# An adaLN and mixture-of-experts block on one core: recurrence steps and residual transposes moved between the output matmuls

## The chip, the cores and the metric

One core of a Trainium2 chip runs the whole block as one program. The metric is device time in microseconds. The program is written engine by engine: TensorE (PE), VectorE (DVE), ScalarE (ACT), GpSimd (POOL) and SyncE (SP) each have their own instruction list, and they meet at semaphores.

## The reference

Two layers follow each other on x of shape (16, 128, 128), 2048 tokens of 128 features.

```python
x = x + ffn0(cond0(x, cond, weight), w_gate, w_up, w_down)
x = x + ffn1(cond1(x, cond, Wx, Wh, b), router_w, w1, b1, w2, b2)

# ffn0: every tensor is quantised to 16 bits with one scale from its largest magnitude
up, gate = act_qdq(x @ up.T), act_qdq(x @ gate.T)
gate = act_qdq(gate * fixed_qdq_u16(sigmoid(gate)))
o = act_qdq(gate * up)
return o @ dequant(w_down).T

# cond1: a recurrence over 128 times, 16 batches side by side
next_h = tanh(xw_t + prev_h @ Wh)

# ffn1: 8 experts of width 512, the best 2 of each token mixed by softmax
h1 = gelu(x @ w1.T + b1);  expert = h1 @ w2.T + b2
```

## The kernel before

Values are kept as pairs of float16 numbers (high and low part), and a product is three or four float16 matmuls, so that nearly float32 accuracy is kept. The 128 times are cut into five chunks of 256, 384, 512, 512 and 384 tokens (`WIDTHS`; below, chunks 0 to 4, "the third chunk" is chunk 2). Both the output of the first layer and the loop of the second go chunk by chunk.

The change touches the stage between the two layers. Its steps for chunk c are:

- Quantise: `quantise_o` on VectorE multiplies the product `up2` by a scale and adds `MAGIC` (line 744, float32 to float32 in place, semaphore `oq`); the rounded 16-bit number then stands in the low bytes. The high byte becomes float16 in `o_hi` (line 746, VectorE). The low byte becomes float16 in `o_lo` through `low_byte`, on ScalarE for the first `LOW_SCALAR` = 3 chunks (line 543) and on GpSimd for the other two (line 393).
- Output: twelve matmuls on TensorE (lines 1031 to 1040) multiply high and low part by the high and low weights; matmuls 0 to 5 need `o_hi`, 6 to 11 need `o_lo` too. Line 893 is the helper that issues every matmul.
- Residual: `make_x1` (line 752, VectorE) scales the output out of PSUM and adds the transposed x; `split_x1` makes the float16 pair (cast, line 759; subtraction, line 761).
- Recurrence: `first_step` on TensorE is a float32 product of `Wh` with the last state, 16 columns; ScalarE's `first_step` takes the tanh (line 555), and the next step waits for it. The first 16 steps (`FIRST_STEPS`) belong to chunk 0 and run in this stage: `input_part` puts the input product of these steps in PSUM, then steps stand after every third output matmul from chunk 2 on (`STEP_EVERY`), and what is left comes behind the last chunk. GpSimd splits the states (lines 404 and 406) and then prepares the bias b2 (lines 411 to 414).
- Residual in token order: `transpose_x1` (line 1017) transposes all sixteen residual tiles behind the steps, four to a PSUM bank. ScalarE copies two banks into the accumulator `acc` (line 563), VectorE the other two (line 779).

Then the loop over experts begins (`pair`): eight slots to an iteration, in each a hidden product on TensorE, Gelu on ScalarE (lines 592 and 594), the float16 pair on VectorE (cast 868, subtraction 872), and from the fifth slot on the down product of the slot four before, for which TensorE waits on `g_lo_done`. Recurrence steps of the next chunk stand between the slots.

The engines' own lists set the order: VectorE goes through quantise 0, quantise 1, residual and split 0, quantise 2, quantise 3, residual and split 1, quantise 4, residual and split 2, residual 3, residual 4, split 3, the bank copies, split 4.

Of the kernel before, what the change touches and what calls it, by code (L numbers as in the profile page):

```python
# [8 lines left out]
ALU = mybir.AluOpType  # L9
ACT = mybir.ActivationFunctionType  # L10
X, XY = mybir.AxisListType.X, mybir.AxisListType.XY

P = 128
B = 16
# [3 lines left out]
NJ = INNER // P  # L18
BANK = 512
NK = TOK // BANK  # L20
# [10 lines left out]
FIRST_STEPS = WIDTHS[0] // B  # L31
RNN_SLOTS = ((0, 1, 3, 4, 5, 7), range(8), range(8), (0, 1, 2, 4, 5, 6), ())
RNN_FROM = [FIRST_STEPS + E // 2 * sum(len(n) for n in RNN_SLOTS[:c]) for c in range(CH)]
# [6 lines left out]
MAGIC = 12582912.0  # L40
# [2 lines left out]
C_SCALAR = (0, 2)  # L43
W_POOL = 8
WARM = 14
STEP_EVERY = 3
LOW_SCALAR = 3
W0_AT = (0, 3, 14)
WY_V = 10
TIMES = [s // B for s in START]  # L50
W_CHUNKS = 2 * E
BH_LO = 32
ACC_SCALAR = 2
CHUNK_OF = [c for c in range(CH) for _ in range(TILES[c])]
LAST_SYNC, LAST_SCALAR = (0, 2), (1,)
LATE = NK - ACC_SCALAR
# [5 lines left out]
def program(nc, x, cond, w_cond, w_gate, w_up, w_down, w_x, w_h, b_h, w_router, w1, b1, w2, b2, out):  # L62
    ctx = ExitStack()
    with ctx:
# [9 lines left out]
        banks = [ctx.enter_context(nc.psum_tensor(f"bank{i}", [P, BANK], F32)) for i in range(8)]  # L74


        ident = sb("ident", [P, P])
# [22 lines left out]
        gate2, up2, sig2 = (big[:, i * NJ * TOK:(i + 1) * NJ * TOK] for i in range(3))  # L100
# [3 lines left out]
        sc = sb("sc", [P, 5, 5])  # L104
# [46 lines left out]
        wt_t = [sem(f"wt_t{i}") for i in range(2)]  # L151
# [64 lines left out]
        def chunk_of(t, c):  # L216

            return t.rearrange("p (jb t) -> p jb t", t=T)[:, :, TIMES[c]:TIMES[c + 1]]
# [5 lines left out]
        def by_batch(c):  # L224

            return banks[DOWN_BANKS[c]][:, 0:WIDTHS[c]].rearrange("p (b t) -> p b t", b=B)
# [222 lines left out]
        def _(act):  # L449
# [91 lines left out]
            def low_byte(c):  # L541
                act.wait_ge(oq, c + 1)
                A(chunk_of(o_lo, c), chunk_of(up2.bitcast(U8)[:, 0::4], c), ACT.Copy).then_inc(o_lo_done, 1)
# [2 lines left out]
            weight_lo(W_CHUNKS - 1)  # L546
            for c in range(1, LOW_SCALAR):
                low_byte(c)
            act.wait_ge(misc_sb, 1)

            def first_step(r):

                act.wait_ge(rnn_mm, r + 1)
                at = slice(r * B, (r + 1) * B)
                A(h32[:, at], ps_rnn[:, at], ACT.Tanh, scale=1 / WS).then_inc(h32_done, 1)  # L555


            act.wait_ge(wt_t[1], 16 * (W_CHUNKS - W_POOL))
            for r in range(FIRST_STEPS):
                first_step(r)  # L560
            for k in range(ACC_SCALAR):
                act.wait_ge(x1T_mm, k + 1)
                A(acc[:, 4 * k:4 * k + 4, :].rearrange("p j h -> p (j h)"), banks[ACC_BANKS[k]][:, :],
                  ACT.Copy).then_inc(acc_s, 1)
# [41 lines left out]
        def _(dve):  # L606
# [134 lines left out]
            peak_to_scale(4, 2 * NJ, lambda u: link(V.tensor_tensor(u, sc[:, 3, 2:3], sc[:, 2, 2:3], ALU.mult)))  # L741
            def quantise_o(c):

                V.tensor_scalar(chunk_of(up2, c), chunk_of(up2, c), sc[:, 4, 4:5], MAGIC, ALU.mult, ALU.add).then_inc(oq, 1)  # L744
                dve.wait_ge(oq, c + 1)
                V.tensor_scalar(chunk_of(o_hi, c), chunk_of(up2.bitcast(I8)[:, 1::4], c), 256.0, None,  # L746
                                ALU.mult).then_inc(o_hi_done, 1)
# [143 lines left out]
        def _(pe):  # L891
            def mm(o, l, r, start, stop=True):
                return nc.tensor.matmul(o, l, r, start=start, stop=stop, skip_group_check=True)  # L893
# [101 lines left out]
            def input_part(first, to):  # L995

                at = slice(B * first, B * to)
                o = ps_rnn[:, 0:B * (to - first)]
                mm(o, bh_rows[:, :], ones[:, 0:B * (to - first)], True)
                mm3(o, wx_hi[:, :], wx_lo[:, :], x1_hi[:, at], x1_lo[:, at], False)  # L1000
# [3 lines left out]
            def first_step(r):  # L1004

                if r:
                    pe.wait_ge(h32_done, r)
                state = h32[:, B * (r - 1):B * r] if r else yT[:, :]
                mm(ps_rnn[:, B * r:B * (r + 1)], w_h32, state, False).then_inc(rnn_mm, 1)

            def transpose_x1(k):

                pe.wait_ge(x1_done, k + 2)
                for j in range(4 * k, 4 * k + 4):
                    last = nc.tensor.transpose(banks[ACC_BANKS[k]][:, P * (j % 4):P * (j % 4 + 1)], x1[:, P * j:P * (j + 1)],  # L1017
                                               ident[:, :])
                last.then_inc(x1T_mm, 1)

            step = 1
            for c in range(CH):
                if c == 2:
                    pe.wait_ge(w_lo_s, W_CHUNKS - W_POOL)
                    pe.wait_ge(small_w, 2)
                    pe.wait_ge(bh_ready, 1)
                    pe.wait_ge(x1_lo_done, 1)
                    input_part(0, FIRST_STEPS)
                    first_step(0)
                pe.wait_ge(o_hi_done, c + 1)  # L1030
                for p, (part, w) in enumerate(((o_hi, wT_hi), (o_hi, wT_lo), (o_lo, wT_hi), (o_lo, wT_lo))):
                    if p == 2:
                        pe.wait_ge(*((o_lo_done, c + 1) if c < LOW_SCALAR else (o_lo_p, c + 1 - LOW_SCALAR)))
                    for j in range(NJ):
                        if c >= 2 and (NJ * p + j) % STEP_EVERY == 1 and step < FIRST_STEPS:
                            first_step(step)
                            step += 1
                        last = mm(by_batch(c), w[:, 2 * NJ + j, :], chunk_of(part, c)[:, B * j:B * (j + 1), :],
                                  p == 0 and j == 0)
                last.then_inc(down_mm, 1)  # L1040

            for r in range(step, FIRST_STEPS):
                first_step(r)
            for k in range(NK):
                transpose_x1(k)

            def transpose_gates(c):

# [50 lines left out]
            def pair(c, e2, prev):  # L1099
                first = is_first(e2)  # L1100
                for s in range(2 * NF):
                    f = s % NF
                    if 0 < c < CH - 1 and first and s == 0:
                        pe.wait_ge(h32_done, RNN_FROM[c])
                        pe.wait_ge(x1_lo_done, CH)
                        input_part(RNN_FROM[c], RNN_FROM[c + 1])

                    if first and s == 0:
                        earlier_slot(c, e2, prev, s)
                    step = rnn_step(c, e2, s)  # L1110
                    if c == 0 and first and s in (2, 3):
                        pe.wait_ge(acc_s, s - 1)
                    if c == 0 and first and s == NF:
                        pe.wait_ge(added, 1)
                    if first and s == 0:
                        pe.wait_ge(h_lo_done, START[c + 1] // (4 * B))

                    if prev or s >= NF:
                        slot = c * SLOTS + e2 * 2 * NF + s
                        two_reads = f in HI_SCALAR[c] or (first and f in HI_SCALAR[c - 1])  # L1120
                        pe.wait_ge(g_lo_done if two_reads else g32_done, slot - NF + 1)
                    t = slice(START[c], START[c + 1])
                    o, w_hi, w_lo = ps_h[f][:, 0:WIDTHS[c]], *(wt_flat[:, w_cols(e2, s, 0, low)] for low in range(2))
                    mm(o, w_hi, h_hi[:, t], True)
                    mm(o, w_lo, h_hi[:, t], False)
                    if step is not None:
                        pe.wait_ge(h32_done, step)
                        mm(ps_rnn[:, bass.ds(rnn_column(c, step), B)], w_h32, h32[:, bass.ds((step - 1) * B, B)],
                           False).then_inc(rnn_mm, 1)
                    mm(o, w_hi, h_lo[:, t], False).then_inc(hid_mm, 1)  # L1130
                    if not (first and s == 0):
                        earlier_slot(c, e2, prev, s)
                    if first and s == 0:
                        if prev:
                            pe.wait_ge(logit_sb, c)
                        logits(c)
                    if first and c > 0 and s == 4:
                        transpose_gates(c - 1)
                    if first and c > 0 and s == 6:
                        mix_b2(c - 1)  # L1140
                    if isinstance(e2, int) and not first and s == 2:
                        transpose_gates(c)
                    if isinstance(e2, int) and not first and s == 4:
                        mix_b2(c)

            pe.wait_ge(h32_done, FIRST_STEPS)
            pe.wait_ge(x1_lo_done, 2)
            input_part(FIRST_STEPS, RNN_FROM[1])
            pe.wait_ge(wt_t[0], 16 * W_POOL)
            pe.wait_ge(wt_t[1], 16 * (W_CHUNKS - W_POOL))  # L1150
            chunks(pe, pair)
# [22 lines left out]
```

## Time and profile before

| | |
|---|---|
| median of 3 runs | 302.65 us (301.67 to 302.88) |
| span of the profiled execution | 301.2 us |
| median less span | 1.45 us |
| PE busy | 264.4 us, 88% |
| DVE busy | 258.8 us, 86% |
| ACT busy | 215.6 us, 72% |
| POOL busy | 76.2 us, 25% |
| stage between the layers | about 81 to 104 us of the span |

The span runs from the first to the last instruction of one profiled execution; its record gives no other time for that execution. Busy shares are of the span. In a timeline a row is a group of like instructions: start, length, engine, line, operation, output and input, shapes, count; square brackets give the idle time ahead of it and who ended it. The names in rows are those of the underlying buffers: `big` holds up2 and the hidden values, `x_sb` the residual's float16 pair, `c` the residual, `wyT` the accumulator, `q` the recurrence states.

### The profile page before, as it was taken

The numbers are of one execution on the slowest core, as the hardware profiler recorded it, in microseconds if no ns is written. First come the engines' busy times: TensorE is split into PE (matmuls) and PEld (weight loads), VectorE is DVE, ScalarE is ACT, GpSimd is POOL, SyncE is SP. The second block draws the span as 40 slices with busy tenths as digits, with TensorE's granted clock in tenths as the row PEclk, the third lists the DMA queues.
The fourth block names the chain that finished last, engine by engine and source line by source line (L and its number), as shares of the span: only waits on it lengthen the run. The fifth ranks groups of instructions, "written<-read, shape, count | busy, mean of one in ns | idle before, by whom it ended". The sixth has DMA issues, their size and how long they took to land.

```text
span 301.2 us, 8834 instructions
## 1 busy us (share of the span) xinstructions
PE 264.4 (88%) x2716; PEld 205.5 (68%) x2716; DVE 258.8 (86%) x635; ACT 215.6 (72%) x455; POOL 76.2 (25%) x148
## 2 busy tenths in 40 slices
PE   4969940049989999999999999999999999999994
PEld 4824440016956777778888788888777887888874
DVE  4888999989898897779988799887799988889885
ACT  6367899998842677767777676667566766689892
POOL 3367997000025413011302112212110311101000
PEclk9989976557999999999999999999999999999999
DMA  6990443101500000000000000000001000001000
GB/s 186 314 310 4 84 94 76 28 0 35 90 17 2 0 3 1 0 2 2 19 0 0 2 3 26 2 0 0 1 2 30 8 0 0 2 1 37 0 2 27
DMA packets 24031, 10.63 MB, mean 35 GB/s; under 512 B 13355, under 2 KB 22982, under 8 KB 24006
## 3 DMA queue, kind: packets, MB, share of 16 engines
q1 hardware_dynamic: 23470, 10.05, 13.6%
q10 hardware_dynamic: 536, 0.26, 0.3%
q8 instruction: 14, 0.23, 0.3%
q14 instruction: 11, 0.09, 0.1%
HBM read 6.11 MB, written 1.05 MB: 24 GB/s over the span
## 4 chain that ended last, share of the span: by engine, by line
PE 79%; DVE 16%; issue 1%; ACT 1%; DMA 1%; SPq 0%; DVEq 0%
PE bank L893 78%; DVE peak L706 3%; DVE big L728 3%; DVE peak L633 2%; DVE big L711 1%; DVE big L744 1%; PE bank L937 1%; DMA y_sb<-in_cond 1%; PE bank L1017 0%; DVE big L746 0%; DVE wyT L779 0%; DVE pkm L626 0%; DVE big L738 0%; DVE x_sb L759 0%; DVE q L700 0%
## 5 line engine op out<-in xcount | busy, mean ns | idle before, releaser
L893 PE MATMUL bank<-big,wt 128*128 128x384 f16 (+2 forms) x480 | 124.8, 336 | 0.6 <-DVE big L872 0.5
L893 PE MATMUL bank<-wt,big 128*128 (+1 forms) x1536 | 111.5, 219 | 0.1
L872 DVE TENSOR_TENSOR big<-big 128x384 f16<-128x384 f32 (+2 forms) x160 | 93.2, 585 | 20.5 <-ACT big L594 16.1
L893 PEld LDWEIGHTS bank<-wt,big 128*128 128x128 f16 x1536 | 97.9, 97 | 16.2 <-issue 0.2
L592 ACT ACTIVATE big<-bank,miscT 128x384 f32<-128x384 f32 (+2 forms) x160 | 96.2, 602 | 15.3 <-PE bank L893 8.2
L893 PEld LDWEIGHTS bank<-q,wxh 128*128 128x128 f32 x254 | 44.4, 189 | 17.4 <-issue 3.4
L893 PEld LDWEIGHTS bank<-big,wt 128*128 (+1 forms) x480 | 50.0, 117 | 4.8 <-issue 1.1
L580 ACT ACTIVATE q<-bank (+1 forms) x112 | 20.6, 184 | 38.7 <-PE bank L893 37.9
L404 POOL CAST big<-q 128x64 f16<-128x64 f32 x32 | 13.2, 413 | 129.0 <-ACT q L580 126.5
L868 DVE CAST big<-big 128x512 f16<-128x512 f32 (+2 forms) x104 | 38.6, 372 | 4.8 <-ACT big L592 3.9
L827 DVE SCALAR_TENSOR_TENSOR wyT<-bank,gates,wyT 128x128 f32<-128x128 f32 x128 | 39.8, 343 | 1.0 <-issue 0.6
L893 PE MATMUL bank<-q,wxh 128*128 (+1 forms) x254 | 38.9, 228 | 1.1 <-ACT q L555 0.7
L594 ACT ACTIVATE big<-bank,miscT 128x384 f16<-128x384 f32 (+2 forms) x56 | 33.1, 590 | 0.0
L893 PE MATMUL bank<-ident,pk 128*128 128x128 f32 x10 | 2.9, 378 | 20.6 <-DVE pk L621 20.6
L893 PE MATMUL bank<-q,wT_hi 128*128 128x512 f16 x48 | 15.8, 398 | 3.0 <-DVE q L698 2.4
L893 PEld LDWEIGHTS bank<-ident,pk 128*128 128x128 f32 x10 | 2.0, 237 | 21.7 <-DVE pk L621 17.4
L506 ACT ACTIVATE big<-bank 128x512 f32<-128x512 f32 x24 | 14.0, 602 | 3.5 <-PE bank L893 2.9
L633 DVE TENSOR_REDUCE peak<-big 128x1 f32<-128x1024 f32 x12 | 14.6, 1219 | 0.4
L706 DVE TENSOR_REDUCE peak<-big 128x1 f32<-128x1536 f32 x8 | 14.0, 1745 | 0.4 <-ACT big L506 0.2
L393 POOL CAST big<-big 128x1536 f16<-128x1536 uint8 (+1 forms) x2 | 3.9, 1962 | 38.9 <-DVE big L744 38.9
L406 POOL TENSOR_TENSOR big<-q,big 128x64 f16<-128x64 f32 x32 | 12.6, 395 | 2.6
L893 PEld LDWEIGHTS bank<-q,wT_hi 128*128 128x128 f16 x48 | 4.8, 101 | 9.8 <-issue 4.1
(165 smaller groups left out, 320.0 us busy)
## 6 DMA issues: line engine op xcount, KB each, us to landing
wnat<-in_w SPq DMA_DIRECT2D x8, 512.0 KB, 7.7
x_sb<-in_x SPq DMA_DIRECT2D x4, 256.0 KB, 4.3
out_block<-wyT SPq DMA_DIRECT2D x15, 64.0 KB
wn<-in_w_gate ACTq DMA_DIRECT2D x1, 192.0 KB, 4.9
wn<-in_w_up SPq DMA_DIRECT2D x1, 192.0 KB, 5.6
wn<-in_w_down SPq DMA_DIRECT2D x1, 192.0 KB, 5.7
b_in<-in_b SPq DMA_DIRECT2D x12, 4.0 KB
wt<-wyT SPq DMA_TRANSPOSE x8, 3.0
```

The source lines that it names most:

```text
L404: G.tensor_copy(h_hi[:, at], h32[:, at]).then_inc(h_hi_done, 1)
L406: G.tensor_tensor(h_lo[:, at], h32[:, at], h_hi[:, at], ALU.subtract).then_inc(h_lo_done, 1)
L506: A(blk(t, j * NK + k), banks[GU_BANKS[n % 5]][:, :], ACT.Copy).then_inc(gu_sb, 1)
L580: A(h32[:, bass.ds(step * B, B)], ps_rnn[:, bass.ds(rnn_column(c, step), B)], ACT.Tanh, scale=1 / WS).then_inc(h32_done, 1)
L592: A(g32[:, f, 0:w], ps_h[f][:, 0:w], ACT.Gelu, bias=bias, scale=1 / WS).then_inc(g32_done, 1)
L594: A(g_hi[:, s // NF, f, 0:w], ps_h[f][:, 0:w], ACT.Gelu, bias=bias, scale=1 / WS).then_inc(g_hi_done, 1)
L633: link(V.tensor_reduce(peak[:, i, n:n + 1], t, X, ALU.max, apply_absolute_value=True))
L706: link(V.tensor_reduce(peak[:, i, k:k + 1], tokens((gate2, up2)[i - 1], k), XY, ALU.max, apply_absolute_value=True))
L827: V.scalar_tensor_tensor(a, ps_y[par][:, P * j:P * (j + 1)], g, a, ALU.mult, ALU.add).then_inc(added, 1)
L868: V.tensor_copy(g_hi[:, par, f, 0:w], g32[:, f, 0:w]).then_inc(hi_v, 1)
L872: V.tensor_tensor(g_lo[:, par, f, 0:w], g32[:, f, 0:w], g_hi[:, par, f, 0:w], ALU.subtract).then_inc(g_lo_done, 1)
L893: return nc.tensor.matmul(o, l, r, start=start, stop=stop, skip_group_check=True)
```

## The change

On TensorE, `STEPS_AT` lists before which output matmuls of each chunk a recurrence step stands: step 0 (with the input part) before matmul 9 of chunk 1, six in each of chunks 2 and 3, three in chunk 4. From matmul 1 of chunk 3 on each step is followed by one transpose of a residual tile, eight in all; tiles 8 to 11 come behind chunk 4, then the input part of the next steps (which stood just before the loop), then tiles 12 to 15. On ScalarE the low byte of chunk 2 goes, and its quantising comes; the wait for the weights' transposes moves behind the steps; it copies three banks, VectorE one. GpSimd takes the low bytes of chunks 2, 3 and 4.

```diff
--- before.py
+++ after.py
@@ -43,14 +43,16 @@
 C_SCALAR = (0, 2)
 W_POOL = 8
 WARM = 14
-STEP_EVERY = 3
-LOW_SCALAR = 3
+STEPS_AT = ((), (9,), (1, 3, 5, 7, 9, 11), (1, 3, 5, 7, 9, 11), (1, 4, 7))
+FILL_FROM = (3, 1)
+Q_SCALAR = 2
+LOW_SCALAR = 2
 W0_AT = (0, 3, 14)
 WY_V = 10
 TIMES = [s // B for s in START]
 W_CHUNKS = 2 * E
 BH_LO = 32
-ACC_SCALAR = 2
+ACC_SCALAR = 3
 CHUNK_OF = [c for c in range(CH) for _ in range(TILES[c])]
 LAST_SYNC, LAST_SCALAR = (0, 2), (1,)
 LATE = NK - ACC_SCALAR
@@ -546,6 +548,7 @@
             weight_lo(W_CHUNKS - 1)
             for c in range(1, LOW_SCALAR):
                 low_byte(c)
+            A(chunk_of(up2, Q_SCALAR), chunk_of(up2, Q_SCALAR), ACT.Copy, scale=sc[:, 4, 4:5], bias=MAGIC).then_inc(oq, 1)
             act.wait_ge(misc_sb, 1)
 
             def first_step(r):
@@ -555,9 +558,9 @@
                 A(h32[:, at], ps_rnn[:, at], ACT.Tanh, scale=1 / WS).then_inc(h32_done, 1)
 
 
-            act.wait_ge(wt_t[1], 16 * (W_CHUNKS - W_POOL))
             for r in range(FIRST_STEPS):
                 first_step(r)
+            act.wait_ge(wt_t[1], 16 * (W_CHUNKS - W_POOL))
             for k in range(ACC_SCALAR):
                 act.wait_ge(x1T_mm, k + 1)
                 A(acc[:, 4 * k:4 * k + 4, :].rearrange("p j h -> p (j h)"), banks[ACC_BANKS[k]][:, :],
@@ -741,7 +744,8 @@
             peak_to_scale(4, 2 * NJ, lambda u: link(V.tensor_tensor(u, sc[:, 3, 2:3], sc[:, 2, 2:3], ALU.mult)))
             def quantise_o(c):
 
-                V.tensor_scalar(chunk_of(up2, c), chunk_of(up2, c), sc[:, 4, 4:5], MAGIC, ALU.mult, ALU.add).then_inc(oq, 1)
+                if c != Q_SCALAR:
+                    V.tensor_scalar(chunk_of(up2, c), chunk_of(up2, c), sc[:, 4, 4:5], MAGIC, ALU.mult, ALU.add).then_inc(oq, 1)
                 dve.wait_ge(oq, c + 1)
                 V.tensor_scalar(chunk_of(o_hi, c), chunk_of(up2.bitcast(I8)[:, 1::4], c), 256.0, None,
                                 ALU.mult).then_inc(o_hi_done, 1)
@@ -1010,39 +1014,46 @@
 
 
 
-            def transpose_x1(k):
-
-                pe.wait_ge(x1_done, k + 2)
-                for j in range(4 * k, 4 * k + 4):
-                    last = nc.tensor.transpose(banks[ACC_BANKS[k]][:, P * (j % 4):P * (j % 4 + 1)], x1[:, P * j:P * (j + 1)],
-                                               ident[:, :])
-                last.then_inc(x1T_mm, 1)
-
-            step = 1
+            def transpose_x1(j):
+
+                if j % 4 == 0:
+                    pe.wait_ge(x1_done, j // 4 + 2)
+                last = nc.tensor.transpose(banks[ACC_BANKS[j // 4]][:, P * (j % 4):P * (j % 4 + 1)], x1[:, P * j:P * (j + 1)],
+                                           ident[:, :])
+                if j % 4 == 3:
+                    last.then_inc(x1T_mm, 1)
+
+            step = filled = 0
             for c in range(CH):
-                if c == 2:
-                    pe.wait_ge(w_lo_s, W_CHUNKS - W_POOL)
-                    pe.wait_ge(small_w, 2)
-                    pe.wait_ge(bh_ready, 1)
-                    pe.wait_ge(x1_lo_done, 1)
-                    input_part(0, FIRST_STEPS)
-                    first_step(0)
                 pe.wait_ge(o_hi_done, c + 1)
                 for p, (part, w) in enumerate(((o_hi, wT_hi), (o_hi, wT_lo), (o_lo, wT_hi), (o_lo, wT_lo))):
                     if p == 2:
                         pe.wait_ge(*((o_lo_done, c + 1) if c < LOW_SCALAR else (o_lo_p, c + 1 - LOW_SCALAR)))
                     for j in range(NJ):
-                        if c >= 2 and (NJ * p + j) % STEP_EVERY == 1 and step < FIRST_STEPS:
+                        if NJ * p + j in STEPS_AT[c]:
+                            if step == 0:
+                                pe.wait_ge(w_lo_s, W_CHUNKS - W_POOL)
+                                pe.wait_ge(small_w, 2)
+                                pe.wait_ge(bh_ready, 1)
+                                pe.wait_ge(x1_lo_done, 1)
+                                input_part(0, FIRST_STEPS)
                             first_step(step)
                             step += 1
+                            if (c, NJ * p + j) >= FILL_FROM and filled < 8:
+                                transpose_x1(filled)
+                                filled += 1
                         last = mm(by_batch(c), w[:, 2 * NJ + j, :], chunk_of(part, c)[:, B * j:B * (j + 1), :],
                                   p == 0 and j == 0)
                 last.then_inc(down_mm, 1)
 
-            for r in range(step, FIRST_STEPS):
-                first_step(r)
-            for k in range(NK):
-                transpose_x1(k)
+            assert step == FIRST_STEPS
+            for j in range(filled, 12):
+                transpose_x1(j)
+            pe.wait_ge(h32_done, FIRST_STEPS)
+            pe.wait_ge(x1_lo_done, 2)
+            input_part(FIRST_STEPS, RNN_FROM[1])
+            for j in range(12, B):
+                transpose_x1(j)
 
             def transpose_gates(c):
 
@@ -1111,7 +1122,7 @@
                     if c == 0 and first and s in (2, 3):
                         pe.wait_ge(acc_s, s - 1)
                     if c == 0 and first and s == NF:
-                        pe.wait_ge(added, 1)
+                        pe.wait_ge(acc_s, ACC_SCALAR)
                     if first and s == 0:
                         pe.wait_ge(h_lo_done, START[c + 1] // (4 * B))
 
@@ -1143,9 +1154,6 @@
                     if isinstance(e2, int) and not first and s == 4:
                         mix_b2(c)
 
-            pe.wait_ge(h32_done, FIRST_STEPS)
-            pe.wait_ge(x1_lo_done, 2)
-            input_part(FIRST_STEPS, RNN_FROM[1])
             pe.wait_ge(wt_t[0], 16 * W_POOL)
             pe.wait_ge(wt_t[1], 16 * (W_CHUNKS - W_POOL))
             chunks(pe, pair)
```

## Rows read from the trace of the kernel before

**Rows 1.** Page: each engine's busy time, share of the span, instructions.

```profile
PE 264.4 (88%) x2716; PEld 205.5 (68%) x2716; DVE 258.8 (86%) x635; ACT 215.6 (72%) x455; POOL 76.2 (25%) x148
```

**Rows 2.** Chain of waits, in order of time: start us, us, what.

```profile
130.26 167.18 PE bank L893 x2006
```

**Rows 3.** Timeline of VectorE, 79.5 to 106: start us, us, engine line op.

```profile
85.40 1.01 DVE L744 TENSOR_SCALAR big<-big,sc 128x1536 f32<-128x1536 f32 x1
86.45 0.96 DVE L746 TENSOR_SCALAR big<-big 128x1536 f16<-128x1536 int8 x1
...
88.38 0.96 DVE L746 TENSOR_SCALAR big<-big 128x1536 f16<-128x1536 int8 x1
...
90.15 0.72 DVE L759 CAST x_sb<-c 128x384 f16<-128x384 f32 x1
...
92.91 1.08 DVE L752 SCALAR_TENSOR_TENSOR c<-bank,pk,xT 128x512 f32<-128x512 f32 x1
...
97.06 0.85 DVE L752 SCALAR_TENSOR_TENSOR c<-bank,pk,xT 128x384 f32<-128x384 f32 x1 [0.87 <-PE bank L893]
97.83 0.41 DVE L759 CAST x_sb<-c 128x512 f16<-128x512 f32 x1
98.28 0.69 DVE L761 TENSOR_TENSOR x_sb<-c,x_sb 128x512 f16<-128x512 f32 x1
...
100.15 1.29 DVE L779 COPY wyT<-bank 128x512 f32<-128x512 f32 x2 [1.18 <-PE bank L1017]
101.36 0.98 DVE L759 CAST x_sb<-c 128x384 f16<-128x384 f32 x1
...
102.84 0.29 DVE L868 CAST big<-big 128x256 f16<-128x256 f32 x1
```

**Rows 4.** Timeline of TensorE, 79.5 to 106.

```profile
84.16 0.66 PE L893 MATMUL bank<-big,wT_hi 128*128 128x384 f16 x3 [0.15 <-DVE big L746]
...
87.47 0.39 PE L893 MATMUL bank<-big,wT_hi 128*128 128x512 f16 x1 [0.41 <-DVE big L746]
...
89.52 0.38 PE L893 MATMUL bank<-big,wT_hi 128*128 128x512 f16 x1
89.73 0.29 PE L893 MATMUL bank<-q,wxh 128*128 128x16 f32 x2
89.87 0.59 PE L893 MATMUL bank<-big,wT_hi 128*128 128x512 f16 x2
...
97.62 0.40 PE L893 MATMUL bank<-q,wxh 128*128 128x16 f32 x2 [0.27 <-ACT q L555]
98.29 0.40 PE L893 MATMUL bank<-q,wxh 128*128 128x16 f32 x2 [0.27 <-ACT q L555]
98.54 1.95 PE L1017 MATMUL bank<-ident,c 128*128 128x128 f32 x16
...
101.18 0.38 PE L893 MATMUL bank<-big,wt 128*128 128x256 f16 x2
...
103.74 0.38 PE L893 MATMUL bank<-big,wt 128*128 128x256 f16 x2 [0.47 <-DVE big L872]
```

**Rows 5.** Timeline of ScalarE, 79.5 to 106: low bytes.

```profile
83.34 1.16 ACT L543 ACTIVATE big<-big 128x1152 f16<-128x1152 uint8 x1
86.45 1.48 ACT L543 ACTIVATE big<-big 128x1536 f16<-128x1536 uint8 x1 [1.95 <-DVE big L744]
```

**Rows 6.** Timelines of GpSimd and VectorE where both are at work.

```profile
46.25 1.16 POOL L351 TENSOR_TENSOR nat<-wnat,nat 128x512 f16<-128x512 f32 x1
46.27 1.68 DVE L711 TENSOR_SCALAR big<-big 128x1024 f32<-128x1024 f32 x1
63.27 0.76 DVE L733 TENSOR_SCALAR big<-big,sc 128x1024 f32<-128x1024 f32 x1
...
88.41 2.25 POOL L393 CAST big<-big 128x1536 f16<-128x1536 uint8 x1 [37.19 <-DVE big L744]
...
100.96 1.15 POOL L414 TENSOR_TENSOR b_diag<-b_in,b_diag 32x512 f16<-32x512 f32 x1
```

## The prediction, made before the changed kernel ran

> **What bounds the kernel now.** I read the page's busy line first: TensorE is busy 88% of the span, VectorE 86%, ScalarE 72%, GpSimd 25% [rows 1]. TensorE is the engine of the span as a whole, but shares are averages over stages, so the next view is the chain of waits. It ends in one unbroken TensorE piece of 167.18 us from 130.26 on [rows 2], and in the stage ahead of the loop, which this change touches, it crosses VectorE for the residual's bank copies and split. The stage ends where the loop's fifth slot starts on TensorE, at 103.74, after 0.47 us of waiting for VectorE's L872 [rows 4]. That slot needs VectorE's first pair (L868 at 102.84, then L872) [rows 3]. The loop's slots are paced alike before and after the change, so every microsecond by which L868 moves should move the end of the kernel by the same amount. The question is only when VectorE reaches its first L868.
>
> Backwards from 102.84, VectorE has: the split of the last residual chunk (from 101.36, its cast alone 0.98), the two copies of residual banks from 100.15, an idle wait of 1.18 us before them for the transposes, and ahead of that the fourth chunk's split (0.41 and 0.69) after the fifth residual chunk (0.85 at 97.06), which itself waits for the last output matmul [rows 3]. So three things hold the stage up: output matmuls, the tail of recurrence steps, the transposes.
>
> The sum is made against the profiled execution, of which the record gives the span, 301.2 us. The median of the timed runs is 302.65 us, 1.45 us more, and I carry that difference over. A change under 0.5% (1.5 us) I call none.
>
> **Term 1, the third chunk's quantising on ScalarE.** ScalarE ends its low byte of the second chunk at 84.50. An operation of the new one's size took 1.48 (the 1536-element low byte at 86.45) [rows 5]. The trace has none of this form and size; I take 1.5, from 84.5 to 86.0, with bounds of 1.2 (the 1.16 of 1152 elements) and 2.0 (a third more). VectorE drops its own 1.01 us (85.40 to 86.41) and its high byte (0.96) runs from 86.05 to 87.0, not from 86.45 to 87.41 [rows 3]. That is 0.4 us earlier. The cover is VectorE's wait of 0.65 us for ScalarE.
>
> **Term 2, the first step in the second chunk.** Nine matmuls of 0.163 us (three of 384 columns in 0.66 with the drain of the last; 0.21 for 512 columns gives 0.16 as well) from 84.16 end at 85.63. The first split residual chunk is there by then, since VectorE goes on to its next operation at 85.40. The input part (four matmuls of 256 columns, about 0.6), step 0 (0.14) and the three matmuls that are left (0.49) end at about 86.9, ahead of the new high byte at 87.0 [rows 3, 4]. So the move costs TensorE nothing. It starts the recurrence 1.3 us earlier, since ScalarE's 1.48 us low byte no longer stands in front of the first tanh. Chunk 2 starts at 87.05 instead of 87.47 [rows 4].
>
> **Term 3, a step every two matmuls.** One 512-column matmul takes 0.21 us of TensorE (89.52 to 89.73) and one step 0.14 (89.73 to 89.87). A step with two matmuls is 0.57. But where a step waits for its tanh the period is 0.67 (97.62 to 98.29), so chunk 2 is bound by the recurrence: 0.2 + 6 x 0.67, ending at 91.25. In chunk 3 a transpose fills the gap: sixteen in 1.95 us is about 0.12 each, so the period is 0.69 and TensorE does not wait. Chunk 4 has 0.75 a step. The three steps exposed behind the last chunk (0.27 us of waiting each) and twelve of the sixteen transposes leave the tail [rows 4].
>
> **Term 4, the low byte on GpSimd.** This is the term that decides. The ordinary length of GpSimd's cast has to be taken apart: it lasts 2.25 us from 88.41, and VectorE's high byte (0.96 at 88.38) runs until 89.34, so 1.32 come after it [rows 3, 6]. That GpSimd and some VectorE operations exclude each other is plain elsewhere. L711 on VectorE, a scalar operation from and to SBUF, took 1.68 us at 46.27 while GpSimd's L351 ran until 47.41; a like one (L733) with GpSimd idle took 0.76 [rows 6]. The cast at 90.15 took 0.72 (384 columns, where 512 took 0.41) and the one at 101.36 took 0.98, both beside GpSimd [rows 3, 6]. In the changed kernel VectorE's quantising of the fourth chunk comes right behind its high byte, at 87.0, exactly where GpSimd's low byte of the third chunk wants the ports. Whichever goes first, one high byte later both are done: 87.0 + 1.2 + 1.0 + 0.96 = 90.15, against 89.34 before. That is 0.8 us later. The low byte is ready at 88.3 to 89.3, and TensorE asks for it at about 89.
>
> The Trainium skill's page "GPSIMD Engine Reference", section "Specifications", says that GpSimd shares its SBUF interfaces with VectorE and contends with its two-port modes and with operations that have two SBUF inputs. The trace agrees in the 1.68 us above; without that rule the result would be the first rival's below.
>
> **Term 5, the residual and TensorE's wait for it.** From the fourth high byte to the end of the third residual chunk there were 4.65 us (89.34 to 92.91 + 1.08) [rows 3]; these operations stay, so it ends at 94.8. TensorE's fifth filled-in transpose needs it, and comes at 91.25 + 0.21 + 4 x 0.69 = 94.2. TensorE then waits 0.6 us, with output matmuls and the recurrence behind it. Chunk 3 ends at 94.85 + 1.05 = 95.9. Chunk 4 is 12 x 0.163, three steps and two transposes, 2.6 us, so 98.55, and its result at 98.7. Before it was 97.06 [rows 3]. So 1.7 us move from the tail to ahead of the last output matmul.
>
> **Term 6, the tail.** VectorE: residual 0.8 from 98.75; fourth split 0.45 + 0.65 to 100.65; one residual copy, not two, 0.6; fifth split 0.4 + 0.5. That is 102.2 without GpSimd. GpSimd's three b2 operations (the last 1.15 at 100.96) follow the last recurrence state and now start almost 1 us earlier and run to about 101.9, across both splits. One wait cost 0.6 before; I take 0.35 and 0.15, with bounds of 0 and 1.4 (both splits stopped for the whole of L414's 1.15 and a part of another) [rows 3, 6]. L868 starts at 102.65, 0.2 us ahead of 102.84. The transposes of the last four tiles (wait for the residual at 99.6, then 0.5) are ready before VectorE asks. ScalarE's third bank copy lies in its idle time before its first Gelu and costs nothing, else 0.5. TensorE itself is ready for the loop at 98.55 + 0.5 (four transposes) + 0.75 (input part of 384 columns) + 0.5 = 100.3, 0.9 ahead of 101.18 [rows 4], and waits at the fifth slot for VectorE.
>
> **Sum.** 102.65 - 102.84 is -0.2 us: 302.45, which I give as 302.4. Of some 3.4 us of exposed steps (3 x 0.67) and transposes (12 x 0.12) that leave the tail, about all comes back, half as chunks 2 to 4 running longer, half as VectorE's own list, which is then what the loop waits for.
>
> **Rivals.**
> First, no collision at the ports: VectorE's L744 and L746 run beside GpSimd at full speed, as L746 seems to at 88.38 (0.96, the same as alone). Then the third residual chunk ends at 93.3, chunk 3 doesn't wait, the last output is at 98.2, and L868 comes at 101.5 with one small b2 collision. That gives -1.4 us, 301.2. Against it stand the 1.68 and 0.98 us rows.
> Second, TensorE decides: VectorE catches up and the gain is TensorE's own 0.9 us, 301.7. Against it: VectorE has no gap from 98.75 on.
> Third, on the slow side: GpSimd takes the ports first when ScalarE's signal releases both engines at 86.05. At 46.25 GpSimd started 0.02 us ahead of VectorE and VectorE waited; at 88.38 VectorE was 0.03 ahead and won, but there the signal was its own [rows 3, 6]. Then the high byte ends at 88.35, chunk 2 starts at 88.4 and, at 0.67 a step, ends at 92.5, later than the residual wait; the last output is at 99.5 and L868 at 103.5. That is +0.6 to +0.8 us, 303.3. It decides from the point at which GpSimd gets its request in before VectorE's. With L414 across both splits it becomes 304.2.
> Fourth, the change doesn't do what it says: if ScalarE's quantising took over 2 us, the high byte would be later than before. The 1.48 us row leaves little room.
>
> **How the numbers follow.** Forecast 0.45; no collision 0.15; TensorE decides 0.10; GpSimd first 0.25, a third of it with the worse tail; rest 0.05. The range to the other cases is 301.0 to 303.9. Faster by over 0.5% (below 301.15) needs the no-collision case and a bit more: 0.17. Slower by over 0.5% (above 304.15) is the worst tail: 0.09. Within: 0.74.
>
> **What would show it.** High byte of the third chunk ending at 87.0 (or 88.3: third rival). L744 of the fourth chunk at over 2 us (or GpSimd's first cast at over 3) against 1.0: term 4. A TensorE wait of about 0.6 us before the fifth transpose: term 5. VectorE without a gap from 98.7 to its first L868 at about 102.7, and TensorE idle for over 1 us before the fifth slot. The forecast is wrong if the last output matmul ends before 98, or if the loop's slots run at another pace than before.

## The result and the profile after

The changed kernel takes 304.66 us (median of 5 runs, 304.38 to 305.20), the kernel before 302.46 in the same comparison. The ratio is 1.0074, 95% interval 1.0054 to 1.0093: 2.2 us slower. I had forecast 302.4, and 301.0 to 303.9 as the range.

Three cuts of the span say where it went. The first row is the time up to VectorE's first quantising, the second the stage up to its first cast of the loop, the third the next 8 us, the last the rest. Columns: start and end, length, then busy us and instructions of PE, PE's weight loads, DVE, ACT and POOL in this order, granted TensorE clock (1.00 is 2.4 GHz, 0.50 is 1.2 GHz), DMA share, GB/s. Before:

```profile
0.00:81.17 81.17, 50.51 (x263) 33.46 (x263) 70.75 (x118) 65.56 (x94) 36.37 (x59) 0.81 0.46 112
81.17:102.84 21.67, 20.36 (x153) 14.40 (x152) 19.14 (x28) 9.54 (x27) 9.05 (x13) 1.00 0.06 13
102.84:110.84 8.00, 7.44 (x90) 6.34 (x89) 7.59 (x35) 5.99 (x20) 1.91 (x4) 1.00 0.01 3
110.84:301.20 190.36, 186.11 (x2217) 151.31 (x2214) 161.36 (x457) 134.52 (x316) 28.84 (x72) 1.00 0.03 7
```

After:

```profile
0.00:80.69 80.69, 49.86 (x263) 32.70 (x263) 70.85 (x117) 65.62 (x94) 36.27 (x59) 0.79 0.45 112
80.69:102.81 22.12, 20.67 (x156) 14.30 (x154) 19.45 (x27) 11.42 (x32) 11.21 (x14) 1.00 0.06 13
102.81:110.81 8.00, 7.04 (x67) 6.16 (x68) 7.47 (x34) 3.70 (x13) 1.01 (x3) 0.79 0.01 3
110.81:302.90 192.09, 187.73 (x2236) 152.75 (x2233) 162.36 (x458) 135.14 (x318) 28.95 (x74) 1.00 0.02 7
```

The stretch up to the stage is the same program in both; over the profiled executions of all runs here it lay between 79.9 and 81.5 us, so it is left out of comparisons. The stage is 0.45 us longer (22.12 against 21.67). From its end to the end of the span there are 200.09 us against 198.36: 1.73 us more, in code that the change does not touch. The clock of the third row says what that is: 0.79. TensorE's timeline shows it slot by slot:

```profile
103.70 0.38 PE L897 MATMUL bank<-big,wt 128*128 128x256 f16 x2 [1.81 <-DVE big L876]
...
104.97 0.64 PE L897 MATMUL bank<-big,wt 128*128 128x256 f16 x2
...
106.49 0.85 PE L897 MATMUL bank<-big,wt 128*128 128x256 f16 x3
...
107.58 0.38 PE L897 MATMUL bank<-big,wt 128*128 128x256 f16 x2
```

These are the fifth to the eighth slot. In the kernel before, the seventh and the eighth stood here:

```profile
105.34 0.49 PE L893 MATMUL bank<-big,wt 128*128 128x256 f16 x3
...
106.00 0.38 PE L893 MATMUL bank<-big,wt 128*128 128x256 f16 x2
```

Three matmuls of 256 columns take 0.85 us where they took 0.49 at full clock, and from the fifth slot to the eighth there are 3.88 us (103.70 to 107.58) against 2.26 before (103.74 to 106.00), 1.62 us more. TensorE had just waited 1.81 us for VectorE, where it had waited 0.47 before [rows 4], and then its clock was at half (1.2 GHz) for 3.4 us. In 2 us stretches the granted clock lacks 0.01, 0.50 and 0.34 of full; that sum times 2 us is 1.7 us lacking, and twice that, since half is lacking at a time, is 3.4 us:

```profile
102.00:104.00 2.00, 0.30 (x4) 0.32 (x5) 1.90 (x8) 0.77 (x3) 0.00 (x0) 0.99 0.00 0
104.00:106.00 2.00, 2.00 (x17) 1.81 (x16) 1.93 (x11) 0.78 (x3) 0.97 (x2) 0.50 0.01 4
106.00:108.00 2.00, 2.00 (x21) 1.80 (x20) 1.86 (x11) 1.10 (x4) 0.00 (x0) 0.66 0.00 0
```

The fall began about 0.25 us after TensorE had resumed. It shows in three more profiled executions below (the changed kernel again, VectorE's list rearranged, the added delay with b2 early): there it began between 0.1 us before TensorE resumed and 0.6 us after, and lasted 3.4 us each time.

The stage itself, VectorE's timeline of the changed kernel (these lines moved down by 4: 744 is now 748, 746 is 750, 752 is 756, 759 is 763, 761 is 765, 779 is 783, 868 is 872), answering to [rows 3]:

```profile
85.52 0.96 DVE L750 TENSOR_SCALAR big<-big 128x1536 f16<-128x1536 int8 x1 [0.51 <-ACT big L551]
86.40 2.22 DVE L748 TENSOR_SCALAR big<-big,sc 128x1536 f32<-128x1536 f32 x1
...
93.18 1.07 DVE L756 SCALAR_TENSOR_TENSOR c<-bank,pk,xT 128x512 f32<-128x512 f32 x1
...
98.26 0.88 DVE L756 SCALAR_TENSOR_TENSOR c<-bank,pk,xT 128x384 f32<-128x384 f32 x1 [1.54 <-PE bank L897]
99.06 0.81 DVE L763 CAST x_sb<-c 128x512 f16<-128x512 f32 x1
99.90 1.52 DVE L765 TENSOR_TENSOR x_sb<-c,x_sb 128x512 f16<-128x512 f32 x1
101.35 0.68 DVE L783 COPY wyT<-bank 128x512 f32<-128x512 f32 x1
101.95 0.34 DVE L763 CAST x_sb<-c 128x384 f16<-128x384 f32 x1
102.33 0.56 DVE L765 TENSOR_TENSOR x_sb<-c,x_sb 128x384 f16<-128x384 f32 x1
102.81 0.28 DVE L872 CAST big<-big 128x256 f16<-128x256 f32 x1
```

and GpSimd's, answering to [rows 6]:

```profile
85.55 2.25 POOL L395 CAST big<-big 128x1536 f16<-128x1536 uint8 x1 [34.82 <-ACT big L551]
88.75 2.19 POOL L395 CAST big<-big 128x1536 f16<-128x1536 uint8 x1 [0.94 <-DVE big L748]
...
98.28 0.61 POOL L413 TENSOR_SCALAR b_in<-b_in 96x512 f32<-96x512 f32 x1
98.97 0.61 POOL L414 TENSOR_SCALAR b_diag<-b_in 96x512 f16<-96x512 f32 x1
99.67 1.21 POOL L416 TENSOR_TENSOR b_diag<-b_in,b_diag 32x512 f16<-32x512 f32 x1
```

The fourth split took 0.81 + 1.52, where it took 0.41 + 0.69 with GpSimd idle: the subtraction, wanted at 99.90, ended 0.54 us after L416 did (99.67 + 1.21 = 100.88).

### The profile page after: what moved, and what is told of

Its sections match the earlier page's. It is cut to its first block, busy times and chain, and to the rows that moved or that the text cites. A ratio compares the mean times of both kernels' runs of the same rounds, so it can differ in the third digit from the quotient of the medians.

```text
span 302.9 us, 8839 instructions
## 1 busy us (share of the span) xinstructions
PE 265.3 (88%) x2716; PEld 205.9 (68%) x2716; DVE 260.1 (86%) x633; ACT 215.9 (71%) x456; POOL 77.4 (26%) x149
## 4 chain that ended last, share of the span: by engine, by line
PE 74%; ACT 12%; DVE 8%; DMA 2%; issue 2%; SPq 0%; DVEq 0%
PE bank L897 74%; ACT big L520 2%; ACT big L518 2%; ACT big L527 2%; ACT big L523 2%; ACT big L534 2%; DMA wn<-in_w_gate 2%; DVE big L748 1%; DVE big L750 1%; DVE c L756 1%; DVE peak L636 1%; DMA y_sb<-in_cond 1%; DVE x_sb L763 1%; ACT xT L468 1%; ACT big L551 0%
## 5 line engine op out<-in xcount | busy, mean ns | idle before, releaser
L406 POOL CAST big<-q 128x64 f16<-128x64 f32 x32 | 12.0, 374 | 131.2 <-ACT q L583 130.2
L872 DVE CAST big<-big 128x512 f16<-128x512 f32 (+2 forms) x104 | 38.8, 373 | 6.0 <-ACT big L595 5.3
L395 POOL CAST big<-big 128x1536 f16<-128x1536 uint8 (+1 forms) x3 | 6.1, 2035 | 37.4 <-ACT big L551 34.8
L897 PE MATMUL bank<-ident,wnat 128*128 128x128 f32 x64 | 11.0, 303 | 0.4 <-ACT wyT L457 0.4
```

The lines of the kernel that those rows point to most:

```text
L406: G.tensor_copy(h_hi[:, at], h32[:, at]).then_inc(h_hi_done, 1)
L872: V.tensor_copy(g_hi[:, par, f, 0:w], g32[:, f, 0:w]).then_inc(hi_v, 1)
```

## The experiments

All are compared with the kernel before, run beside them on the same chip (its medians there: 302.66 to 302.89). "Stage" is, in the profile, from VectorE's first quantising to its first cast of the loop; "rest" from there to the end. Before has 21.67 and 198.36, changed 22.12 and 200.09. "Wait" is TensorE's, before the loop's fifth slot. Stage, rest, wait and clock are seen in one profiled execution of each kernel; how often a fall comes can only be read from the times. Diffs are cut to the lines that matter, with "..." where lines are left out.

**Is it the clock?** "Clock theory" below means: the long wait lets TensorE's clock fall, and the slots behind it run at half clock. First, TensorE's wait filled with work that serves nothing:

```diff
                         pe.wait_ge(acc_s, ACC_SCALAR)
+                        for _ in range(7):
+                            mm(banks[1][:, :], wT_hi[:, 0, :], wT_hi[:, 0:4, :].rearrange("p j o -> p (j o)"), True)
```

> The changed kernel with seven matmuls of 512 columns that compute nothing (into a free bank) between the loop's fourth and fifth slot, where TensorE sat idle for 1.81 us. Clock theory: the idle wait let TensorE's clock fall to half for the next three slots, which cost 1.6 us; with the wait filled (7 x 0.213 = 1.5 us) the clock stays at its full level, slots 5 to 8 run at 0.8 us each, and the time falls by 1.4 to 1.7 us against the changed kernel, to about 303.1. Rival, the wait alone: VectorE's late arrival is the whole loss and the slow slots are bound by something else; then nothing changes (304.7), or it is slower if the seven push the fifth slot back.

303.11 us, ratio 1.0016 (1.0001 to 1.0032). Stage 22.11 as in the changed kernel, rest 198.55. Its 8 us behind the stage, columns as above:

```profile
103.35:111.35 8.00, 7.72 (x89) 6.20 (x87) 7.55 (x36) 4.70 (x16) 1.44 (x4) 1.00 0.01 3
```

Full clock, and about 1.5 us back (304.69 to 303.11, by the ratios 1.0065 to 1.0016), by adding work. The fall is what cost the slots their time, and what is left is the stage's 0.45 us.

With `range(2)` in place of `range(7)`:

> The changed kernel with two (not seven) idle matmuls of 512 columns before the fifth slot: TensorE's wait is 1.4 us in place of 1.81. If the fall needs the full wait, the clock stays up and the time is about 303.1, like with seven. If any wait over about 1 us does it, 304.7.

303.33 us, ratio 1.0024 (1.0007 to 1.0040), wait 1.29 us, rest 198.37. All twelve executions were at or below 303.73. Two such matmuls are enough:

```profile
102.53:110.53 8.00, 7.01 (x86) 6.09 (x86) 7.55 (x36) 4.71 (x16) 1.42 (x4) 1.00 0.01 3
```

The changed kernel with no edit:

> The changed kernel once more, beside the kernel before on this chip, to see whether the fall of the clock comes each time. If it does, 304.7 us, ratio 1.006 to 1.009, and three slots at half clock after the wait of 1.8 us. If it was one look's accident, 303.1.

304.69 us, ratio 1.0065 (1.0042 to 1.0087). Wait 1.81, rest 199.78, and the clock fell again. Eleven of twelve executions were at 303.66 or above, one at 302.29. That suggests that the fall comes in most executions; it does not count them, since the kernel before spread from 301.32 to 304.21 beside them.

**Is the wait alone enough?** The kernel before, with VectorE made late:

```diff
             dve.wait_ge(acc_s, ACC_SCALAR)
+            link(V.tensor_reduce(pkm[:, 0:1], xT[:, 0:1024], X, ALU.max))   # 0:1536 in the second; a branch that is never taken is left out here
```

> The kernel before with one VectorE reduction of 1024 elements (1.25 us, result unused) ahead of its first L868, so that TensorE waits 1.7 us before the fifth slot in place of 0.47. Clock theory: the time rises by 1.25 + 1.5 = 2.8 us, to about 305.2, with three slots at half clock. Rival, linear: 1.25 us more, 303.7.

304.00 us, ratio 1.0040 (1.0026 to 1.0055): 1.1 us more, about the 1.25 us by which the stage grew (22.92). The clock theory missed here. TensorE waited 1.72 us and kept its clock:

```profile
102.81:110.81 8.00, 7.00 (x85) 6.01 (x86) 7.59 (x34) 4.67 (x16) 2.05 (x4) 1.00 0.01 3
```

With `xT[:, 0:1536]`:

> The kernel before with a VectorE reduction of 1536 elements (1.75 us) ahead of its first L868, so a wait of 2.2 us. Linear: 302.9 + 1.75 = 304.6. Clock: with this longer wait (1.72 us did not do it) three slots at half clock on top, 306.2.

304.19 us, ratio 1.0054 (1.0031 to 1.0078), wait 2.25 us, rest 198.36:

```profile
103.54:111.54 8.00, 7.00 (x85) 6.06 (x86) 7.58 (x34) 4.61 (x15) 2.03 (x4) 1.00 0.01 3
```

Ten executions lay between 303.2 and 304.61, two at 306.4. So the clock theory as I had put it, by the length of the wait, fell here: a longer wait than the changed kernel's mostly cost its own length and no more.

And in the changed order of work, with the same added line (`0:1024`) on the changed kernel whose b2 operations are moved early (their diff is below):

> The changed kernel with b2 moved early (302.2 us, wait 0.58 us, no fall of the clock) and one VectorE reduction of 1.25 us ahead of the first cast, so that the wait before the fifth slot is 1.83 us again, as in the changed kernel, by another cause. If the wait in this order of work lets the clock fall: 302.2 + 1.25 + 1.7 = 305.1 in most executions. If the port collisions are needed for it: 303.4.

304.42 us, ratio 1.0046 (1.0026 to 1.0066), 0.7 us below my number. Wait 1.83 us, stage 22.12, rest 199.99, and eleven of twelve executions at 303.65 or above (one at 302.09). Its 8 us:

```profile
102.01:110.01 8.00, 7.03 (x67) 6.19 (x68) 7.48 (x33) 3.75 (x13) 0.93 (x3) 0.79 0.01 3
```

So the collisions with b2 are not needed for the fall: in the changed order of TensorE's work a wait of 1.8 us was followed by it in these profiled executions, whether b2 or an added operation made VectorE late. In the order before, waits of 1.72 and 2.25 us mostly were not. The length of the wait does not settle it even in the changed order, as `e8_order_alone` below shows.

**The port collisions.** By this I mean the rows in which a VectorE operation takes longer beside a GpSimd one. The runs show the delay and what it goes with; that both engines need the same ports is the prediction's reading, and nothing here shows the ports themselves. GpSimd's b2 operations moved to where VectorE alternates with reductions, one beside each:

```diff
+                pool.wait_ge(p_done, 1)   # 2 and 3 ahead of the second and third operation
                 link(G.tensor_scalar(b2_in[:, :], b2_in[:, :], WS, 0.0, ALU.mult, ALU.add))
...
-            split_b2()                    # was behind the first four split_states; now ahead of low_byte
```

> The changed kernel with GpSimd's three b2 operations moved into its idle time at 64 to 70 us, each beside a VectorE reduction. Port theory: the fourth split (0.81 + 1.52 us in the changed kernel) falls back to 0.41 + 0.69, VectorE reaches its first L872 about 1.2 us earlier, TensorE's wait before the fifth slot falls from 1.81 to about 0.6 to 0.8, and with it the fall of the clock goes: 1.2 + 1.6 = 2.8 us less, about 301.9. Rival, wait and clock independent: only 1.2 us less, 303.5. Rival, no collision: no change, 304.7.

302.18 us, ratio 0.9969 (0.9955 to 0.9982). Stage 20.88, 1.24 less than the changed kernel's; wait 0.58; full clock; rest 198.58. The fourth split (lines 768 and 770 here) is back at its old length:

```profile
99.29 0.42 DVE L768 CAST x_sb<-c 128x512 f16<-128x512 f32 x1
99.75 0.69 DVE L770 TENSOR_TENSOR x_sb<-c,x_sb 128x512 f16<-128x512 f32 x1
```

The same edit on the kernel before:

> The kernel before with GpSimd's b2 operations moved in the same way. Port theory: the cast at 101.36 (0.98) falls to 0.36, VectorE's first L868 is 0.6 us earlier: 301.9. Rival: no change (302.5). If the moved operations collide with VectorE's products at 64 to 70 us it is slower than that by up to 1 us.

302.17 us, ratio 0.9976 (0.9962 to 0.9990), stage 21.25, 0.42 less than before. With b2 out of the way the changed kernel and the kernel before are equal to 0.1% (302.18 and 302.17). So the change is worth nothing once b2 is moved, and costs 2.2 us where it is not.

VectorE's list rearranged in the changed kernel, and then in the one with b2 early:

```diff
-                if c in (1, 3):
-                    make_x1(c // 2)
-                    split_x1(c // 2)
+                if c == 1:
+                    make_x1(0)
+                    split_x1(0)
+                if c == 2:
+                    make_x1(1)
+                if c == 3:
+                    split_x1(1)
```

> The changed kernel with VectorE's second residual chunk (reads PSUM, 0.86 us, no second SBUF port) between the third chunk's high byte and the fourth's quantising, so that it runs beside GpSimd's low byte. Port theory: the quantising falls from 2.22 to about 1.4 us, but GpSimd's next low byte then stops the following cast longer; the third residual chunk comes 0 to 0.6 us earlier, the time is 0 to 0.6 us less than the changed kernel's. Rival (the quantising is slow for another reason, such as ScalarE's in-place write): it stays at 2.2 us.

304.75 us, ratio 1.0056 (1.0036 to 1.0077). VectorE:

```profile
86.99 0.88 DVE L756 SCALAR_TENSOR_TENSOR c<-bank,pk,xT 128x384 f32<-128x384 f32 x1
87.78 1.20 DVE L748 TENSOR_SCALAR big<-big,sc 128x1536 f32<-128x1536 f32 x1
...
89.89 1.62 DVE L763 CAST x_sb<-c 128x384 f16<-128x384 f32 x1
```

The quantising fell from 2.22 to 1.20 us once it no longer began beside GpSimd's low byte, so it is not slow for a reason of its own. But the cast behind it rose from 0.73 to 1.62: the next low byte stopped that instead. Stage 22.11, rest 199.83 with the clock's fall, nothing gained.

> The same reorder with the b2 operations moved early: 302.2 us (the b2 version's) less 0 to 0.6 us.

302.11 us, ratio 0.9981 (0.9964 to 0.9997), stage 20.89: again nothing from the reorder.

**Which part of the change.** Two halves. The first is the kernel before with

```diff
-LOW_SCALAR = 3
+LOW_SCALAR = 2
...
+            A(chunk_of(up2, 2), chunk_of(up2, 2), ACT.Copy, scale=sc[:, 4, 4:5], bias=MAGIC).then_inc(oq, 1)
...
-                V.tensor_scalar(chunk_of(up2, c), chunk_of(up2, c), sc[:, 4, 4:5], MAGIC, ALU.mult, ALU.add).then_inc(oq, 1)
+                if c != 2:
+                    V.tensor_scalar(chunk_of(up2, c), chunk_of(up2, c), sc[:, 4, 4:5], MAGIC, ALU.mult, ALU.add).then_inc(oq, 1)
```

> The kernel before with only the change of engines: the third chunk quantised by ScalarE, its low byte on GpSimd; TensorE's list as before. Port theory: high byte 0.4 us earlier, then the fourth chunk's quantising stands 1.2 us behind GpSimd (2.2 us in place of 1.0) and the third residual chunk is 0.8 us later, but TensorE's list does not ask for it early, so the stage is as long as before to 0.2 us: 302.9. Rival (the engines' part is a gain by itself): 0.4 us less or more.

302.51 us, ratio 0.9992 (0.9975 to 1.0008), stage 21.33. The quantising took 2.22 us here too, and nobody waited for it: TensorE's list asks for no residual tile before the steps are done.

The second is the changed kernel with

```diff
-Q_SCALAR = 2
-LOW_SCALAR = 2
+Q_SCALAR = -1
+LOW_SCALAR = 3
...
-            A(chunk_of(up2, Q_SCALAR), chunk_of(up2, Q_SCALAR), ACT.Copy, scale=sc[:, 4, 4:5], bias=MAGIC).then_inc(oq, 1)
```

> The changed kernel with the engines as before: TensorE's new order alone, quantising of the third chunk on VectorE and its low byte on ScalarE. By the recurrence chain: the first tanh again stands behind ScalarE's 1.48 us low byte, steps in chunk 2 follow at 0.67 us each, so chunk 2 ends about 1.2 us later than in the changed kernel; against that the port collision at the fourth chunk is gone. Last output 1 to 2 us later than in the changed kernel, time 305 to 306.5 with the clock's fall. Rival (ports decide): 304 or less.

304.73 us, ratio 1.0067 (1.0040 to 1.0095); stage 22.47, wait 1.81. My number for chunk 2 was too pessimistic, the last output came only 0.4 us later than in the changed kernel, relative to the stage's start. The profiled execution kept its clock (rest 198.60), with the same wait of 1.81 us and the same order of TensorE's work as the changed kernel, where it fell:

```profile
103.10:111.10 8.00, 7.02 (x85) 6.15 (x86) 7.58 (x35) 4.67 (x15) 1.91 (x4) 1.00 0.01 3
```

The twelve executions fall in two groups, six from 302.69 to 304.18 and six from 305.29 to 305.85; that the upper group is the one with the fall is an inference from the times. So this half has the whole loss, though not by quite the same shares: a stage longer by 0.8 us, and a fall in about half of the executions. Besides TensorE's new order it keeps the third bank copy on ScalarE and the later wait for the weights' transposes, which were not tested by themselves.

**A version that beats both.** Engines of the quantising and pace of the steps as before (but the first step stays in chunk 1, and ScalarE still copies three banks), b2 early, and transposes only in chunk 4 and where a step waits. On the changed kernel, with the two diffs for b2 and for the engines as above:

```diff
-STEPS_AT = ((), (9,), (1, 3, 5, 7, 9, 11), (1, 3, 5, 7, 9, 11), (1, 4, 7))
+STEPS_AT = ((), (9,), (1, 4, 7, 10), (1, 4, 7, 10), (1, 4, 7, 10))
-FILL_FROM = (3, 1)
+FILL_FROM = (4, 1)
...
-            assert step == FIRST_STEPS
+            for r in range(step, FIRST_STEPS):
+                first_step(r)
+                for _ in range(2):
+                    transpose_x1(filled)
+                    filled += 1
```

> A version meant to beat both: engines as before the change (quantising on VectorE, three low bytes on ScalarE, two on GpSimd), steps after every third matmul as before but the first one in chunk 1, a transpose behind each step of chunk 4 and two behind each of the three exposed steps (whose 0.27 us waits they fill), then tiles 10 and 11, the input part and the last four; one bank copy on VectorE; b2 moved into GpSimd's idle time. Port and chain theory: the last output is 0.3 us later than before, the stage is 1.7 to 2.0 us shorter (L868 at about 100.9 in place of 102.84), TensorE hardly waits before the fifth slot: 300.9 us. Rival (the time is TensorE's own list, whose work stays the same): no better than b2 alone, 302.2.

302.45 us, ratio 0.9990 (0.9975 to 1.0004), stage 21.17, no difference from before. A miss: VectorE was done with its fourth split early, and then waited for tiles 12 to 15, which stood behind the input part:

```profile
100.82 0.69 DVE L787 COPY wyT<-bank 128x512 f32<-128x512 f32 x1 [1.44 <-PE bank L1025]
```

Then tiles 12 to 15 ahead of the input part, and VectorE's fifth split ahead of its bank copy:

```diff
-            for j in range(filled, 12):
+            for j in range(filled, B):
                 transpose_x1(j)
             pe.wait_ge(h32_done, FIRST_STEPS)
             pe.wait_ge(x1_lo_done, 2)
             input_part(FIRST_STEPS, RNN_FROM[1])
-            for j in range(12, B):
-                transpose_x1(j)
...
             split_x1(CH - 2)
+            split_x1(CH - 1)
             dve.wait_ge(wt_t[1], 16 * (W_CHUNKS - W_POOL))
...
-            split_x1(CH - 1)
             dve.wait_ge(acc_s, ACC_SCALAR)
```

> The combined version once more, with the last four residual tiles transposed ahead of the loop's first input part and VectorE's fifth split ahead of its bank copy, so that VectorE's 1.44 us wait for the transposes is filled. VectorE theory: first cast at 100.9 in place of 102.28 of the combined version; TensorE's own list then sets the fifth slot at about 102.5, and waits no longer: 0.7 us less than 302.45, about 301.8, ratio 0.997 against before. Rival (nothing left to gain once TensorE's list is the limit): 302.4.

301.65 us, ratio 0.9958 (0.9939 to 0.9976): 1.2 us below the kernel before (302.83 there) and 3 below the changed one. Stage 20.67, rest 198.49. Between the loop's fourth and fifth slot TensorE hardly waits any more (0.05 us), and VectorE waits for ScalarE's first Gelu:

```profile
99.32 0.68 DVE L788 COPY wyT<-bank 128x512 f32<-128x512 f32 x1
100.91 0.29 DVE L876 CAST big<-big 128x256 f16<-128x256 f32 x1 [0.91 <-ACT big L599]
```

## Why the prediction was wrong

The stage began 0.48 us earlier in the profile after (80.69 against 81.17), so 0.48 is taken off the predicted moments. Up to TensorE's readiness for the loop the working came true almost to the row; it failed at its last two steps.

- Term 1, right: high byte of the third chunk predicted to end at 86.52, ended at 86.48. ScalarE took 1.56 us.
- Term 2, right: chunk 2 predicted from 86.57, began at 86.54.
- Term 3, right: 0.67 us a step in chunk 2 (87.34, 88.00, 88.67), 0.72 in chunk 3 (0.69 predicted).
- Term 4, right: L748 took 2.22 us beside GpSimd, "over 2" predicted; fourth high byte ended at 89.61, predicted 89.67. The reorder shows that the delay goes with GpSimd's cast.
- Term 5, right: third residual chunk ended at 94.25 (94.3 predicted), TensorE stood still for 0.37 us (0.6 predicted), VectorE began the fifth residual chunk, behind the last output, at 98.26 (98.27 predicted).
- Term 6, in part right: TensorE came to the loop at 99.80 (99.82 predicted). Mis-sized: the collision with b2 was put at 0.35 + 0.15 us. It was 0.40 in the cast and 0.83 in the subtraction, 1.2 in all (moving b2 away gave 1.24). That is inside its stated bounds of 0 to 1.4, and makes the stage 0.45 longer where I had 0.2 shorter: L868, now L872, began at 102.81, 0.64 us after the predicted 102.17.
- The step that failed: "The loop's slots are paced alike before and after the change, so every microsecond by which L868 moves should move the end of the kernel by the same amount." The slots were not paced alike. I had worked out that TensorE would be ready 0.9 us earlier and then wait for over 1 us, and took that wait as costing nothing. With the mis-sized collision it was 1.81 us, and the clock fell to half for the next 3.4 us, which cost 1.73 us. That is 1.73 of the 2.2 us; the filled wait shows it (1.5 us back), and b2 moved early shows it again (1.24 us of VectorE removed, 2.5 us gained by the medians, 2.9 by the ratios). The two failures hang together: with term 6 as predicted the wait would have been about 1.2 us (an estimate: fifth slot at 102.17 + 0.9, TensorE free at 101.89), and with a wait of 1.29 us `e9_fill_two` kept its clock.
- Two slips without effect on the sum. The sentence behind it lets twelve transposes leave the tail; eight do, the other eight stand behind the last output (98.06 and 99.36), as term 6 itself counts them. And the worst case of the third rival, 304.2, lies outside the stated range of 301.0 to 303.9.

Of the rivals, the third (GpSimd first at the ports, 303.3 or 304.2) came nearest in time, but mostly by luck: VectorE got the ports first (85.52 against 85.55), and only its addition, the worse collision with b2, came true in part. The clock stood in no rival. The prediction did name "if the loop's slots run at another pace than before" as a sign that it is wrong, and that is what happened, but it gave this no price and no chance. Before the stage the chip had already shown it: up to 81.17 the granted clock averages 0.81.

What stays open is why a wait of 1.8 us mostly lets the clock fall in the new order of TensorE's work and a wait of 2.25 us mostly doesn't in the old. The new order with the quantising's engines as before seems, by its times, to have had it in about half of the executions. Whether it is the transposes spread between the steps, the moment at which the wait falls, or the work just ahead of it was not taken apart.

## What to carry to other kernels

Making one engine ready earlier than the engine it waits for does not shorten anything, and on TensorE it can lengthen: the idle time is moved into one long wait, and the clock may be at half behind it (here 1.81 us of waiting, then 3.4 us at half clock, 1.7 us lost). Count a wait before a dense TensorE loop as its length plus a possible fall, and fill it or leave the work where it was. Before moving work to GpSimd, or moving VectorE's work in time, lay the two timelines over each other: here the quantising, the casts and the subtractions of VectorE that began beside a GpSimd operation were delayed by about that operation's remainder (1.01 to 2.22 us, 0.41 to 0.81, 0.69 to 1.52), its reductions and its reads out of PSUM were not, and relieving one operation moved the delay to the next.

## What the runs showed that was not expected

- Adding seven useless matmuls to the changed kernel made it 1.5 us faster (304.69 to 303.11, each beside the kernel before).
- GpSimd's three small b2 operations, 2.4 us of work, cost the changed kernel 2.5 us or more where they stood (about half of it through the clock), and nothing beside VectorE's reductions at 65 to 71 us, which they didn't slow (1.22 us each).
- A recurrence step that had to wait for its tanh had a period of 0.67 us, whether two matmuls of 512 columns or nothing stood in it.
